# Windowed attention on one core: loads regrouped, the division by the sum in two halves, and part of the row statistics moved from VectorE to ScalarE

## The reference, cut to what matters

```python
q = Wq @ layernorm(x); k = Wk @ ctx; v = Wv @ ctx      # x, ctx: (16, 64 channels, 512 times)
# 8 heads of 8 channels; each time t looks at 16 neighbours t-8 .. t+7 of k and v
dots[h,t,w] = sum_d q[h,d,t] * k[h,d,t+w-8] * scale
out[h,d,t]  = sum_w softmax_w(dots)[h,t,w] * v[h,d,t+w-8]
x = x + tanh(g_xattn[0]) * (Wo @ out + bo)
```

## Time and profile before

| | |
|---|---|
| median of 3 runs | 1097.15 us (1096.7 to 1097.34) |
| profiled execution | 1095.16 us, of which the span is 1093.0 us |
| mean granted clock of PE | 0.969 of full speed |
| PE busy over the span | 1015.4 us (93%) |
| DVE, ACT, POOL busy | 693.7, 425.8, 549.6 us |
| windowed attention | from 0 to about 242.5 us |

### The profile page before, as it was taken

The page is one execution under the profiler, slowest core; times in us unless marked ns, Lnnn a source line. Parts: engine busy times, 40 slices in busy tenths (PEclk is TensorE's granted clock), DMA queues, the critical chain, the costliest instruction groups (busy, mean ns, idle before and its releaser), DMA issues. The chain is left out here.

```text
span 1093.0 us, 13751 instructions
## 1 busy us (share of the span) xinstructions
PE 1015.4 (93%) x4712; PEld 732.9 (67%) x4712; DVE 693.7 (63%) x1107; ACT 425.8 (39%) x1226; POOL 549.6 (50%) x396
## 2 busy tenths in 40 slices
PE   5688888879779999999999999999999979999998
PEld 1344443446467777777777777777777757888787
DVE  4899998878855776666667677765555552222223
ACT  3233333223214555455555454454534541212121
POOL 3566666545727667657766678653441120313021
PEclk9899999889888999999999999999999998999999
DMA  8000000002122434334433444420101005120002
GB/s 276 1 1 1 0 1 1 1 22 71 38 54 96 131 114 136 91 98 137 139 97 105 147 164 143 131 91 30 44 25 38 1 1 162 40 57 15 1 1 77
DMA packets 60964, 75.93 MB, mean 69 GB/s; under 512 B 8444, under 2 KB 44068, under 8 KB 60888
## 3 DMA queue, kind: packets, MB, share of 16 engines
q1 hardware_dynamic: 56032, 57.66, 16.7%
q0 software_dynamic: 4144, 17.04, 5.1%
q10 hardware_dynamic: 720, 0.36, 0.1%
HBM read 64.37 MB, written 10.68 MB: 69 GB/s over the span
## 5 line engine op out<-in xcount | busy, mean ns | idle before, releaser
L798 PE MATMUL ps<-xh,wqh 128*128 128x512 f32 (+1 forms) x432 | 176.2, 408 | 6.6 <-PEq L1289 5.1
L800 PE MATMUL ps<-xh,wql 128*128 128x512 f32 (+1 forms) x432 | 170.2, 394 | 0.0
L799 PE MATMUL ps<-xl,wqh 128*128 128x512 f32 (+1 forms) x432 | 169.2, 392 | 0.0
L1431 POOL TENSOR_TENSOR shared<-shared 128x512 f32<-128x512 f32 x64 | 87.7, 1370 | 143.2 <-DVE shared L1592 142.5
L1507 ACT ACTIVATE c_xn<-c_xn,c_mn 128x64 f32<-128x64 f32 x256 | 85.9, 337 | 90.8 <-DVE c_mn L1606 90.8
L798 PE MATMUL ps<-woh,oh 128*128 128x512 f32 x256 | 103.4, 404 | 4.3 <-DVE ol L1618 4.3
L1590 DVE TENSOR_TENSOR shared<-ps,cs 128x512 f32<-128x512 f32 x80 | 55.3, 691 | 79.7 <-PE ps L800 75.1
L398 POOL TENSOR_TENSOR r<-r 128x1024 f32<-128x1024 f32 x32 | 76.2, 2380 | 53.7 <-DVE r L610 53.6
L798 PEld LDWEIGHTS ps<-xh,wqh 128*128 128x128 f32 (+1 forms) x432 | 81.2, 188 | 31.7 <-issue 14.8
L799 PE MATMUL ps<-wol,oh 128*128 128x512 f32 x256 | 101.5, 396 | 0.0
L800 PE MATMUL ps<-woh,ol 128*128 128x512 f32 x256 | 101.3, 396 | 0.0
(11 more groups left out here) (182 smaller groups left out, 2174.0 us busy)
## 6 DMA issues: line engine op xcount, KB each, us to landing
stage<-in_wq SPq DMA_DIRECT2D x16, 512.0 KB
stage<-in_wo SPq DMA_DIRECT2D x16, 512.0 KB
w_wide<-dq SPq DMA_DIRECT2D x32, 172.0 KB, 2.7
stage<-w_wide SPq DMA_DIRECT2D x20, 256.0 KB, 3.0
qraw<-in_gate_qweight SPq DMA_DIRECT2D x16, 172.0 KB
qraw<-in_up_qweight SPq DMA_DIRECT2D x16, 172.0 KB
qraw<-in_down_qweight SPq DMA_DIRECT2D x10, 256.0 KB
w_down<-dq SPq DMA_DIRECT2D x10, 256.0 KB, 2.5
```

Source lines behind the costliest of these rows:

```text
L798: pe.matmul(dst, lh, rh, start=(first and c == 0), stop=False)
L799: pe.matmul(dst, lh, rl, start=False, stop=False)
L800: last = pe.matmul(dst, ll, rh, start=False, stop=(final and c == chunks - 1))
L1431: pool.tensor_tensor(qT[:, h * TPH:(h + 1) * TPH, :, p - 1, :], turn(ra), turn(rb), ALU.add)\
```

## The change

1. **Loads.** `W4`, `bias` and `gates` become one array `packed`, loaded by ACT's queue as its only DMA (five before); `sel` and `spread` become one, and it and `ident` go to SP's queue behind the second pair of chunks. SP's second DMA is now the first context chunk.
2. **First layer norm.** Chunks 0, 1, 2 keep their own `statistics`, before the loop; those of 3 to 7 come together in step 0 (five bn_stats, five bn_aggr, one addition, one POOL `pow` of five columns). In steps 1 to 5 ACT, and no longer DVE, normalises chunk `s+2`, at the end of its step, as rstd*x + shift.
3. **Statistics of the finished rows.** `output_out` also gives the sum of each row (`accum_out`), and ACT's new `squares_of_rows` (a Copy of one column, then a Square of 512 with `accum_out`, which writes the free PSUM bank `M`) gives the squared deviations. DVE's `next_sums` and the bn_aggr of the next norm are gone.
4. **Division in halves.** `att` is written in two instructions of 8 windows, and `high_half(i, 0)` waits for the first only.
5. **Products.** POOL does part 1, DVE parts 0, 2, 3.
6. **Order of ACT.** `keys`, `values` and the two `high_half` come ahead of `output_out`; `scores_out(s, 0)` comes between the two `turned_half`; the squares come ahead of `scores_out(s, 1)`. In the prologue the queries come ahead of the values.
7. **Order of PE.** `keys_values(s+1)` lies inside `output(s-2)`, behind its second pair. Group (0, 0) of `reduce_heads` comes ahead of `turn_back(i, 0)`, group (0, 1) behind it, the other two after windows 5 and 8; `scores_turned(s)` comes after window 11 and `queries(s+1)` after 14.

```diff
-            sp.dma_start(w4[:, :, :], a["W4"].rearrange("p (j c) -> p j c", j=4)).then_inc(w4_landed, 16)
             sp.dma_start(ctxt[:, 0, :], cr[0:P, :]).then_inc(ctx_landed[0], 16)
             for i in range(1, NT):
                 ...
+                if i == 1:
+                    sp.dma_start(sel_spread[:, :], a["sel_spread"]).then_inc(tables_landed, 16)
+                    sp.dma_start(ident[:, :], a["ident"]).then_inc(tables_landed, 16)
...
-                        pool.wait_ge(prod_used, 2 * s)
-                    products(pool, q[:, :], s, PART_LAST).then_inc(last_prod_ready, 1)
+                        pool.wait_ge(prod_used, 2 * s - 1)
+                    products(pool, q[:, :], s, POOL_PART).then_inc(pool_prod_ready, 1)
...
-                act.activation(x[:, i, :], M, ACT.Identity, bias=gbo[:, 0:1]).then_inc(x_ready, 1)
+                act.activation(x[:, i, :], M, ACT.Identity, bias=gbo[:, 0:1], accum_out=sums[:, i:i + 1]).then_inc(sums_ready, 1)
+
+            def squares_of_rows(i):
+                act.wait_ge(sums_ready, i + 1)
+                act.activation(mv[:, i, 0:1], sums[:, i:i + 1], ACT.Copy, scale=1.0 / D).then_inc(mean_ready, 1)
+                act.wait_ge(mean_ready, i + 1)
+                act.activation(M, x[:, i, :], ACT.Square, scale=-1.0, bias=mv[:, i, 0:1], accum_out=squares[:, i:i + 1])\
+                   .then_inc(squares_ready, 1)
+
+            def normalise(i):
+                act.wait_ge(shift_ready, 1)
+                if i >= 2:
+                    act.wait_ge(q_done, i - 1)
+                act.activation(xn[:, i % 2, :], x[:, i, :], ACT.Identity, scale=rstd[:, i:i + 1], bias=shift[:, i:i + 1])\
+                   .then_inc(xn_ready, 1)
...
+            def next_variances(first, last):
+                dve.wait_ge(squares_ready, last)
+                dve.tensor_scalar(veps[:, first:last], squares[:, first:last], 1.0 / D, EPS, ALU.mult, ALU.add).then_inc(next_var, 1)
...
-                    dve.tensor_tensor(att[:, :, :, :], T_win,
-                                      rs[:, :, :].unsqueeze(2).broadcast_to([P, D // P, WIN, BH]), ALU.mult)\
-                       .then_inc(att_ready, 1)
+                    for h in range(2):
+                        if s >= 2:
+                            dve.wait_ge(lo_ready, 2 * (i - 1) + h + 1)
+                        windows = slice(h * HALFW, (h + 1) * HALFW)
+                        dve.tensor_tensor(att[:, :, windows, :], T_win[:, :, windows, :],
+                                          rs[:, :, :].unsqueeze(2).broadcast_to([P, D // P, HALFW, BH]), ALU.mult)\
+                           .then_inc(att_ready, 1)
                 if s < NT:
-                    part_of_products(s, 1)
-                if s + 2 < NT:
-                    statistics(s + 2)
+                    part_of_products(s, 2)
+                if s == 0:
+                    part_of_products(s, 3)
+                    statistics(3, NT)
+                    normalise(2)
+                    dve.wait_ge(rstd_ready, 4)
+                    dve.scalar_tensor_tensor(shift[:, 3:NT], mv[:, 3:NT, 0], -1.0, rstd[:, 3:NT], ALU.mult, ALU.mult)\
+                       .then_inc(shift_ready, 1)
...
-                if s < NT:
-                    part_of_products(s, 2)
-                if s + 2 < NT:
-                    normalise(s + 2)
+                if 1 <= s < NT:
+                    part_of_products(s, 3)
...
                 for pair in range(WIN // 4):
+                    if pair == 2 and i + 3 < NT:
+                        keys_values(i + 3)
                     pe.wait_ge(rsum_ready, 4 * i + pair + 1)
...
                 if 1 <= s <= NT:
+                    if s < NT:
+                        reduce_heads(s, 0, 0)
                     turn_back(i, 0)
                     if s < NT:
-                        reduce_heads(s, 0, 0)
+                        reduce_heads(s, 0, 1)
```

More of the change, by code:

```diff
@@ L354, in _, with scale_of_rows @@
             pool.wait_ge(half_set, 1)
-            def scale_of_rows(i):
-                pool.wait_ge(var_ready, i + 1)
-                pool.tensor_tensor(rstd[:, i:i + 1], veps[:, i:i + 1], mhalf[:, i:i + 1], ALU.pow).then_inc(rstd_ready, 1)
+            def scale_of_rows(first, last, groups):
+                pool.wait_ge(var_ready, groups)
+                pool.tensor_tensor(rstd[:, first:last], veps[:, first:last], mhalf[:, first:last], ALU.pow).then_inc(rstd_ready, 1)
             def next_scales(first, last, groups):
@@ L476, in _ @@
                         norm_high(act, g, n1, XT1, k)
+                if s + 1 < NT:
+                    keys(s + 1)
+                    values(s + 1)
+                if 1 <= s <= NT:
+                    high_half(i, 0)
+                    high_half(i, 1)
                 if s >= 2:
                     output_out(s - 2)
-                if s + 1 < NT:
-                    keys_values(s + 1)
+                    if s >= NT:
+                        squares_of_rows(s - 2)
                 if 1 <= s <= NT:
-                    act.wait_ge(att_ready, s)
-                    high_half(i, 0)
-                    high_half(i, 1)
                     if s == NT:
@@ L497, in _ @@
                         queries(s + 1)
+                    if 1 <= s and s + 2 < NT:
+                        normalise(s + 2)
         @block.vector
@@ L508, in link, with statistics @@
                 dve.wait_ge(dve_step, chain[0])
-            def statistics(i):
-                dve.wait_ge(x_landed[i], 16)
-                link(dve.bn_stats(stats[:, i, :], x[:, i, :]))
-                link(dve.bn_aggr(mv[:, i, :], stats[:, i, :]))
-                dve.tensor_scalar(veps[:, i:i + 1], mv[:, i, 1:2], EPS, None, ALU.add).then_inc(var_ready, 1)
+            def statistics(first, last):
+                for i in range(first, last):
+                    dve.wait_ge(x_landed[i], 16)
+                    done = dve.bn_stats(stats[:, i, :], x[:, i, :])
+                link(done)
+                for i in range(first, last):
+                    done = dve.bn_aggr(mv[:, i, :], stats[:, i, :])
+                link(done)
+                dve.tensor_scalar(veps[:, first:last], mv[:, first:last, 1], EPS, None, ALU.add).then_inc(var_ready, 1)
             def normalise(i):
-                dve.wait_ge(rstd_ready, i + 1)
+                dve.wait_ge(rstd_ready, min(i, 3) + 1)
                 if i >= 2:
@@ L529, in part_of_products @@
                 products(dve, QB, i, part).then_inc(prod_ready, 1)
-            def next_sums(i):
-                dve.wait_ge(x_ready, i + 1)
-                row_sums(dve, g, st, i)
-            def next_variances(first, last, groups):
-                dve.wait_ge(st["sums_done"], last)
-                for k in range(first, last):
-                    done = dve.bn_aggr(mv[:, k, :], stats[:, k, :])
-                done.then_inc(aggr_done, 1)
-                dve.wait_ge(aggr_done, groups)
-                dve.tensor_scalar(veps[:, first:last], mv[:, first:last, 1], EPS, None, ALU.add).then_inc(next_var, 1)
+            def next_variances(first, last):
+                dve.wait_ge(squares_ready, last)
+                dve.tensor_scalar(veps[:, first:last], squares[:, first:last], 1.0 / D, EPS, ALU.mult, ALU.add).then_inc(next_var, 1)
             def next_row(i):
@@ L617, in _, with keys_values @@
             pe.wait_ge(w4_landed, 16)
-            def keys_values(i):
+            def keys_values(i, only=(1, 2)):
                 pe.wait_ge(ctx_landed[i], 16)
@@ L703, in spread_window @@
                   .then_inc(spread_done, 1)
-            keys_values(0)
+            keys_values(0, only=(1,))
             queries(0)
-            pe.wait_ge(tables_landed, 48)
+            keys_values(0, only=(2,))
+            pe.wait_ge(tables_landed, 32)
             for s in range(NT + 2):
```

120 lines of the change are left out of this document (64 added, 56 removed).

## The result

| | before | after |
|---|---|---|
| median | 1096.93 us (the three runs quoted above and one of 1092.75) | 1063.88 us (4 runs, 1063.51 to 1064.51) |
| ratio | | 0.9714, interval 0.9696 to 0.9732 |
| profiled execution, span | 1095.16, 1093.0 us | 1063.51, 1061.7 us |
| mean granted clock | 0.969 | 0.982 |
| next layer's first normalisation starts | 242.74 us | 213.80 us |

The change saves 2.9%, 33 us.

A forecast was written before the change was run, and what follows sets the result against it. DVE has least slack now and PE, close behind, would set the changed period; start -1.5, step 1 -1.6, steps 2 to 6 -18.3, step 7 -4.0, end +0.6 give -24.8 us: 1097.15 to 1072.4, range 1066.5 to 1084.

The forecast's parts named there:

- PE's chain in the steady step: Steps 2 to 6: PE's chain from the output's first product ends last by 0.4 us; period 22.4 us, -18.3 in total.
- Step 7: The step without a key product: DVE's 22.1 us stand against 26.1, -4.0 us.
- The start: Up to the first maximum: earlier context DMA and queries before values move it from 25.72 to 24.2 us, -1.5.
- Step 1: From 26.57 us: DVE loses 2 us of statistics and normalisation, groups and turn run partly at half clock; 25.0, -1.6.
- The end: Step 8 and the last output: row variances reach DVE later, +0.2, and ACT's accumulator chain replaces bn_stats, +0.4; together +0.6 us.
- What follows the layer is untouched; I let it shift as a block: Everything behind the layer: PE has nearly the full clock there, so its length changes by 0 us.
- The profiled execution: Base of the sum: rows from an execution of 1095.16 us, 2.0 below the median; the difference was applied to 1097.15.
- The lower bound: Low end of the range, 1066.5 us: the period at DVE's bare 21.7 us and the start at -2.5.
- 1 (PE with its old defects): PE becomes the bound; half-clock stretches and pauses between windows stay in five steps: +11 us, 1083; chance 0.17.
- 2 (the steps keep their length): DVE's freed time turns wholly into waiting; only start and end change: 1096.3 us; chance 0.05.
- 3: Slower: later queries hold up POOL's part of the products, and PE behind it, in seven steps: about 1101 us; chance 0.04.
- 4: Two table loads of 1.28 us a step around each Square on ACT: +7, 1079 us; chance 0.04.

The follow-up runs named there:

- spare reciprocal: Changed kernel with one more reciprocal of 64 columns, its result unused, on DVE ahead of the windows in steps 1 to 7: 1065.33 us, ratio 0.9731.
- missing identity product: Changed kernel without PE's product of the identity with x in the output, which leaves out the addition of x: 1061.1 us, ratio 0.9698.
- spare matmuls: Changed kernel with six spare products of queries into the free bank M in PE's pauses of steps 0 and 1: 1063.82 us, ratio 0.9714.

## Why the prediction was right in kind and 8 us short

**PE's chain in the steady step: right.** The output starts 0.83 us ahead of the maximum (-0.8), output, keys and values take 9.54 (9.45), the first spread comes 11.96 behind the maximum (11.9), DVE's first window 12.56 (12.45). From the first spread to the next maximum it is 10.58 (10.4). 22.55 against 22.4, five times: +0.7 of the error. Step 7 was 22.02 against 22.1. That PE's chain is last, by about half a microsecond where 0.4 was forecast, is what the spare reciprocal and the missing identity product show, in both directions. One reading under it was too simple: the forecast says that PE falls to 1.2 GHz behind its pause of 2.65 us. In step 3 it does (the turn back at 88.37 and what follows it). But steps 2 and 5 have the same pause at a clock of 1.00, and so has every step with the keys behind the output, with 1.65. What decides between the two is open.

**The start, "its DMA is issued one DMA earlier, 0.46 us": failed.** The product came 2.1 us earlier, and the kernel with the new loads alone does the same (7.10 to 5.20) and has its first maximum 2.1 us earlier. I priced the place in the queue and nothing else of the regrouping. Missed: 1.5 us in the traced execution. With the same code the first maximum ranges from 21.95 to 24.26 us, and my 24.2 is in that range, so how much of the 1.5 is the landing and how much the clock in the first scores isn't separated. Nor is what holds up the context: four DMAs fewer on ACT's queue, or `W4` gone from in front of it on SP's, wasn't tried.

**Step 1, "its groups and turn run partly at half clock: 25.0": mis-sized.** It took 23.52. With the groups in their old places it is 25.93, with PE kept busy 22.05, and in the other traces of the changed kernel's order 23.16 to 24.41: all of them under 25.0. So the step's length goes by PE's order and pauses, and I added the new order's gain only for the full clock. Missed: 1.45 us.

**The end, "+0.6 us": wrong sign.** The accumulator chain cost less (0.24 for 0.4), but the last output now runs at 2.4 GHz (201.96, four products in 1.88 us; 2.73 before). I had read the clock for the steps and not for the end. Missed: 1.8 us. About 0.8 of it hangs on the execution: with this output partly at 1.2 GHz and the rest unchanged, the end takes 33.64 us (spare matmuls), which is still 0.4 less than before and not 0.6 more.

**"What follows the layer is untouched; I let it shift as a block": failed.** It took 2.4 us less. About 1.0 of it lies up to the beginning of the third layer and 1.4 at the beginning of the fourth. The windows view shows both, first for the kernel before and then for after, each pair of windows over the same 20 us counted from the start of the next layer:

```profile
300.00:320.00 20.00, 15.70 (x65) 12.52 (x66) 9.28 (x17) 2.65 (x5) 2.98 (x3) 0.81 0.28 74
902.70:922.70 20.00, 18.59 (x76) 14.96 (x76) 5.78 (x10) 4.52 (x8) 2.54 (x2) 0.86 0.62 195
```

```profile
271.00:291.00 20.00, 15.94 (x70) 12.90 (x71) 10.25 (x19) 3.50 (x7) 3.11 (x3) 0.91 0.28 74
873.80:893.80 20.00, 18.59 (x85) 15.17 (x85) 6.05 (x10) 4.52 (x8) 2.54 (x2) 0.96 0.69 218
```

The clock reads 0.81 and 0.86 there before and 0.91 and 0.96 after, for the same code. Over all thirteen traces the stretch behind the layer lies between 847.9 and 851.3 us, though none changes anything in its instructions. The shortest is that of the changed kernel; its nine variants read 848.5 to 851.3, the kernel before and its two variants 850.3 to 850.5. So much of the 2.4 us is luck, and no run shows that any of it is the edit's. What decides where the slow stretches fall is open.

**The profiled execution.** I took the difference of the profiled spans and applied it to the median. The profiled run of before is 1.8 us under its median, and single runs of it lie up to 4.6 us apart; no step of the sum could have held that, and the range should have. These 1.75 us are luck too.

These misses (1.5, 1.45, 1.8, 2.4, and 1.75 between spans and medians) add up to 8.9, and less the 0.7 in the steps to 8.2 us. The distance to the median of 1063.88 is 8.5, and the base, 1097.15 for 1096.93, gives 0.2. All of them but the steps' went one way, and about half of the 8.9 (2.4, 1.75 and part of the end) belongs to the executions that were traced or timed and not to the change. The lower bound held only DVE's bare chain and a start of -2.5, which are worth 4.9 us by the forecast's own figures where the bound lies 5.9 below the forecast; step 1, the end, the layers behind and the spread of the runs had no lower side in it.

**The rivals.** 1 (PE with its old defects) is refuted by the clock of 1.00 and by windows with one pause, of 0.22 us, among them. 2 (the steps keep their length) is what the statistics do alone, and it didn't happen because the order changed with them. 3: POOL's part 1 starts at 93.78 and ends at 97.95, 2.1 us ahead of PE's group, as the slack was counted. 4: the rival was two loads around each Square. By the Trainium skill, "ScalarE: Activation LUTs", Table sets, Square is not listed among the fillers of each set. One load of 1283 ns stands in the whole trace, with Squares between exponentials, so here Square shares the set of the exponential.

**The sum of the parts.** From the changed kernel, taking back one part costs in the medians 10.2 us (statistics), 10.7 (keys and values), 10.8 (groups), 2.8 (division); from the kernel before, the statistics alone give 0 and the loads alone 2.7. With the loads they add up to 37 us, where 33 were saved, and each of these differences holds a share of a few microseconds that the traces don't tie to the edit. Three chains lie close together (PE 22.55, DVE 22.0, the rounding and turning back 0.6 us off PE). Taking back the statistics lengthens the second, the keys' place the third and the groups' place what follows the turn back, and any one of them alone takes the step off PE's own sum.

## What to carry to other kernels

Where a wait already follows the busiest engine in one step of its timeline, taking work from that engine gave nothing until the engine it waits for was reordered. Adding up the second chain from its first instruction, as it would be ordered, gave the period to a per cent. Ask of a moved instruction not only whether the sum on its own engine changes, but what its consumer has queued behind it: the same matmuls 3.4 us later cost 1.7 us a step, through two biases on ACT ahead of the rounding. And give the clock a term of its own in the range, at both ends of the stage and behind it: the four products at the head of the last output took 1.88 us in the changed kernel's trace and 2.76 in that of the variant with the keys behind, whose code there is the same, and the same start took 21.95 to 24.26 us.

## What the runs showed of the hardware

- Untouched code behind a changed stage took 847.9 to 851.3 us in thirteen traces. With a shift of 1.18 us ahead of it it took 3.4 us longer in one execution, with one of 2.37 us 0.6 longer. A difference of 2 us between single executions of two kernels of this program says nothing of the edit by itself.
- The same code up to the first maximum took 21.95 to 24.26 us in eight traces, and the length follows PE's clock: 32 matmuls in 3.84 us in the fastest, in 6.8 in the slowest.
- `accum_out` shows as an instruction of its own (ACTIVATION_READ_ACCUMULATOR), 192 and 187 ns; the ACTIVATE in front of it keeps its 0.69 us. A Copy of one column is 196 ns.
- An Identity of 512 elements with scale and bias both from a column takes 810 ns, against 684 with the bias alone. The first reads SBUF and the second PSUM; the Square, which reads SBUF and has the bias alone from a column, takes 692.
